# Unread products and a four-bank score rotation in the last head group of a macaron transformer layer

## The reference

```
x = x + 0.5 * ffn(ln(x))
x = x + attn(ln(x))          # 16 heads of 16, rotary embedding, causal softmax, output projection
x = x + 0.5 * ffn(ln(x))     # the same weights as the first

ffn(u):  prev = u shifted by one row, zeros first
         xk = mu_k*u + (1-mu_k)*prev ;  xr = mu_r*u + (1-mu_r)*prev
         k = xk @ W_k.T ; r = sigmoid(xr @ W_r.T)
         return r * (square(relu(k)) @ W_v.T)
```

## Time and profile before

| | |
|---|---|
| median of 3 runs | 3127.63 us (3127.12 to 3133.78) |
| profiled execution, its own time | 3128.23 us |
| its span, first to last instruction | 3126.5 us |
| mean granted TensorE clock | 0.986 |
| PE busy over the span | 2973.8 us, 95% |
| DVE, ACT, POOL busy over the span | 80%, 69%, 50% |

### The profile page before, as it was taken

The page is one execution under the profiler, slowest core; times in us unless marked ns, Lnnn a source line. Parts: engine busy times, 40 slices in busy tenths (PEclk is TensorE's granted clock), DMA queues, the critical chain, the costliest instruction groups (busy, mean ns, idle before and its releaser), DMA issues.

```text
span 3126.5 us, 57247 instructions
## 1 busy us (share of the span) xinstructions
PE 2973.8 (95%) x18245; PEld 1667.7 (53%) x18245; DVE 2511.6 (80%) x8326; ACT 2159.5 (69%) x4802; POOL 1566.1 (50%) x2190
## 2 busy tenths in 40 slices
PE   6899999999999999999999999999999999999987
PEld 5444555555555555555555555555555555555434
DVE  3888888888888888888888888888888888888862
ACT  4476677776777777777776777777777676777664
POOL 5455455555454455555555455455555555454322
PEclk8899999999999999999999999999999999999998
DMA  3443243443334253343343334243343433343411
GB/s 99 78 86 65 63 98 68 85 88 75 83 76 91 64 100 73 69 97 68 85 88 74 83 77 92 64 100 74 69 96 69 83 88 75 83 76 79 78 45 38
DMA packets 202593, 245.56 MB, mean 79 GB/s; under 512 B 68405, under 2 KB 104245, under 8 KB 202293
## 3 DMA queue, kind: packets, MB, share of 16 engines
q1 hardware_dynamic: 202293, 241.90, 37.3%
HBM read 53.48 MB, written 51.38 MB: 34 GB/s over the span
## 4 chain that ended last, share of the span: by engine, by line
PE 69%; DVE 15%; ACT 7%; issue 4%; POOL 3%; DMA 1%; SPq 1%; POOLq 0%; DVEq 0%; ACTq 0%
PE ps_y L720 15%; PE ps_s L689 13%; PE ps_m L699 11%; DVE ps_m L926 7%; PE ps_d L779 7%; PE ps_d L773 6%; PE ps_d L785 5%; PE ps_d L776 5%; ACT pt_sb L815 4%; PE ps_d L766 3%; PE ps_d L727 2%; PE ps_d L789 2%; DVE dif_sb L956 1%; DVE ka_sb L950 1%; DVE sw_sb L979 1%
## 5 line engine op out<-in xcount | busy, mean ns | idle before, releaser
L815 ACT ACTIVATE pt_sb<-ps_s 128x512 f32<-128x512 f32 (+3 forms) x3072 | 1464.8, 494 | 839.8 <-PE ps_s L689 829.7
L926 DVE CUSTOM_DVE_ANT_0 ps_m<-ps_m,mask_sb 128x512 f32<-128x512 f32 (+3 forms) x3072 | 1676.1, 570 | 446.9 <-PE ps_m L699 429.7
L689 PE MATMUL ps_s<-qr_sb,kr_sb 99*128 99x512 bf16 (+3 forms) x3072 | 1008.2, 331 | 55.1 <-ACT pt_sb L815 42.7
L699 PE MATMUL ps_m<-kr_sb,qr_sb 96*128 96x512 bf16 (+3 forms) x3072 | 1000.5, 329 | 42.6 <-DVE mx_sb L926 38.0
L1057 POOL TENSOR_SCALAR_AFFINE_SELECT pt_sb<-pt_sb 128x512 f32<-128x512 f32 x512 | 330.7, 646 | 845.1 <-ACT pt_sb L815 844.1
L720 PE MATMUL ps_y<-pt_sb,v_sb 128*32 128x512 f32 (+3 forms) x6144 | 593.4, 496 | 1.2 <-POOL pt_sb L1057 1.2
L689 PEld LDWEIGHTS ps_s<-qr_sb,kr_sb 99*128 99x128 bf16 x3072 | 294.8, 96 | 527.2 <-issue 233.8
L699 PEld LDWEIGHTS ps_m<-kr_sb,qr_sb 96*128 96x128 bf16 x3072 | 302.0, 98 | 325.9 <-DVE mx_sb L926 96.9
L926 DVE DVE_READ_ACCUMULATOR2_ANT mx_sb<- 128x1 f32 x3072 | 431.6, 140 | 0.0
L785 PE MATMUL ps_d<-axn_sb,wqk_sb 128*128 128x256 f32 x1024 | 306.1, 397 | 4.0 <-ACT axn_sb L857 3.9
L773 PE MATMUL ps_d<-ka_sb,wk_sb 128*128 128x256 f32 x1024 | 305.6, 395 | 1.0 <-DVE ka_sb L950 0.9
(11 more groups left out here) (92 smaller groups left out, 3273.7 us busy)
## 6 DMA issues: line engine op xcount, KB each, us to landing
kr_sb<-part_sb SPq DMA_DIRECT2D x378, 128.0 KB, 4.4
qr_sb<-part_sb SPq DMA_DIRECT2D x378, 128.0 KB, 4.7
y_way<-yt_sb SPq DMA_DIRECT2D x128, 256.0 KB, 2.7
sw_sb<-qb_sb SPq DMA_DIRECT2D x496, 64.0 KB, 2.0
x_sb<-x SPq DMA_DIRECT2D x64, 256.0 KB, 2.8
yn_sb<-y_way SPq DMA_DIRECT2D x64, 256.0 KB
den_sb<-r_way SPq DMA_DIRECT2D x64, 256.0 KB
out<-x_sb SPq DMA_DIRECT2D x64, 256.0 KB, 2.2
```

Of the source, the lines that this page charges most:

```text
L689: eng.matmul(ps_s[:, slot % NS, 0:width], kr_sb[0:KR + NP, n % RS, j, kb * P:(kb + 1) * P], qr_sb[0:KR + NP, n % RS, j, q0:q0 + width], st ...
L699: eng.matmul(ps_m[:, u % NM, 0:width], qr_sb[0:KR, n % RS, j, i * P:(i + 1) * P], kr_sb[0:KR, n % RS, j, piece * QC:piece * QC + width], s ...
L815: eng.activation(pt_sb[:, buffer, j, column:column + width], ps_s[:, slot % NS, 0:width], ACT.Exp, scale=SCALE).then_inc(exped, 1)
L926: eng.tensor_tensor_reduce(ps_m[:, u % NM, 0:width], ps_m[:, u % NM, 0:width], mask_sb[:, m0:m0 + width], 1.0, -3e38, ALU.add, ALU.max, mx ...
```

## The change

In the last group and the eight slots ahead of it (from slot 3016, `LONE`), the scores go round four banks, the two of `ps_s` and the first two of `ps_m`, so that a score waits for the exponential of four slots before. The third bank of `ps_m` takes products that nobody reads: `keep_going(n)` issues n matmuls of the form of `f_K` (128 x 128 by 128 x 256, fp32). There is one ahead of each score from slot 3016 on (56), four behind T124 and T126, two behind T125 and T127, and six behind the last matmul of p_P 63. In the planner, the lags of the last batch element's chunks 124 and 125 are halved, `xp` counts as one slot's lag for all four chunks, and p_P 62 and 63 are due at slots 3036 and 3038 with a lag of 1 behind `y_mul`, which ranks them ahead of the feed-forward steps. The outputs are computed as before.

```diff
-            came = ("xp", i, 2) if second else ("load", i, 8 if b else 0)
+            came = ("xp", i, 1 if b == nb - 1 else 2) if second else ("load", i, 8 if b else 0)
+            near = (lambda lag: math.ceil(lag * 0.5)) if second and b == nb - 1 and c < NCH // 2 else (lambda lag: lag)
...
-            s("POOL", "f_rstd", p, 1.3, t, ("f_st1", p, 3), ("f_x1", p - 2, 1))
-            s("ACT", "f_x0", p, 0.36, t, ("f_rstd", p, 4))
+            s("POOL", "f_rstd", p, 1.3, t, ("f_st1", p, near(3)), ("f_x1", p - 2, 1))
+            s("ACT", "f_x0", p, 0.36, t, ("f_rstd", p, near(4)))
...
-            s("PE", "f_T", p, 0.5, t, ("f_x1", p, 2))
+            s("PE", "f_T", p, 0.5, t, ("f_x1", p, near(2)))
...
-                t = (b + 1) * BSLOTS - 16 + 8 * c + 12 * (c // 2)
-                s("PE", "p_P", i, 4, t, ("y_mul", NQC * (b * NP2 + NP2 - 1) + c // 2, 3))
+                last = b == nb - 1 and c >= NCH // 2
+                t = nb * BSLOTS - 40 + 2 * c if last else (b + 1) * BSLOTS - 16 + 8 * c + 12 * (c // 2)
+                s("PE", "p_P", i, 4, t, ("y_mul", NQC * (b * NP2 + NP2 - 1) + c // 2, 1 if last else 3))
...
+        LONE = n_ticks * G - GSLOTS - 8
+        N_LONE = NS + NM - 1
+
+        def score_bank(slot):
+
+            if slot < LONE:
+                return ps_s[:, slot % NS, :]
+            at = (slot - LONE) % N_LONE
+            return ps_s[:, at, :] if at < NS else ps_m[:, at - NS, :]
...
-                pe.wait_ge(exped, slot - NS + 1)
-                eng.matmul(ps_s[:, slot % NS, 0:width], kr_sb[0:KR + NP, n % RS, j, kb * P:(kb + 1) * P],
+                if slot < LONE + NS:
+                    pe.wait_ge(exped, slot - NS + 1)
+                elif slot < LONE + N_LONE:
+                    pe.wait_ge(max_taken, n_groups * NU)
+                else:
+                    pe.wait_ge(exped, slot - N_LONE + 1)
+                eng.matmul(score_bank(slot)[:, 0:width], kr_sb[0:KR + NP, n % RS, j, kb * P:(kb + 1) * P],
...
+            def keep_going(times):
+
+                pe.wait_ge(max_taken, n_groups * NU)
+                for _ in range(times):
+                    eng.matmul(ps_m[:, NM - 1, 0:C], wk_sb[:, 0, 0:P], wk_sb[:, 1, :], start=True, stop=True)
...
                 if name == "f_T":
                     pe.wait_ge(f_xt, CT * (i + 1))
                     transposes(ps, xt_sb).then_inc(made[d], 1)
+                    b, c, second = plan.ffn[i]
+                    if second and b == nb - 1:
+                        keep_going(2 if c % 2 else 4)
                     return
...
                     if u == CT * NP2 - 1:
                         mm.then_inc(made[d], 1)
+                        if i == nb * NCH - 1:
+                            keep_going(6)
...
                 if slot in SCORE_AT:
+                    if slot >= n_ticks * G - GSLOTS - 8:
+                        keep_going(1)
                     score(SCORE_AT[slot])
```

More of the change, by code:

```diff
@@ L129, in describe @@
             i = b * NCH + c
-            came = ("xp", i, 2) if second else ("load", i, 8 if b else 0)
+            came = ("xp", i, 1 if b == nb - 1 else 2) if second else ("load", i, 8 if b else 0)
+            near = (lambda lag: math.ceil(lag * 0.5)) if second and b == nb - 1 and c < NCH // 2 else (lambda lag: lag)
             s("DVE", "f_st0", p, 0.33, t, came, ("f_st1", p - 1, 0))
             s("DVE", "f_st1", p, 0.51, t, ("f_st0", p, 0), ("f_x1", p - 2, 1))
-            s("POOL", "f_rstd", p, 1.3, t, ("f_st1", p, 3), ("f_x1", p - 2, 1))
-            s("ACT", "f_x0", p, 0.36, t, ("f_rstd", p, 4))
+            s("POOL", "f_rstd", p, 1.3, t, ("f_st1", p, near(3)), ("f_x1", p - 2, 1))
+            s("ACT", "f_x0", p, 0.36, t, ("f_rstd", p, near(4)))
             s("ACT", "f_x1", p, 0.36, t, ("f_x0", p, 0))
-            s("PE", "f_T", p, 0.5, t, ("f_x1", p, 2))
+            s("PE", "f_T", p, 0.5, t, ("f_x1", p, near(2)))
             s("ACT", "f_xn", p, 0.48, t, ("f_T", p, 1), ("f_r1", p - 2, 1), ("f_dif", p - 1, 1))
-            s("POOL", "f_dif", p, 1.2, t, ("f_xn", p, 2), ("f_R", p - 2, 1), ("f_xadd", p - 2, 1))
-            s("DVE", "f_k0", p, 0.62, t, ("f_dif", p, 2), ("f_V", p - 2, 1))
+            s("POOL", "f_dif", p, 1.2, t, ("f_xn", p, near(2)), ("f_R", p - 2, 1), ("f_xadd", p - 2, 1))
+            s("DVE", "f_k0", p, 0.62, t, ("f_dif", p, near(2)), ("f_V", p - 2, 1))
             s("DVE", "f_k1", p, 0.62, t, ("f_k0", p, 0))
@@ L142, in describe @@
             s("DVE", "f_r1", p, 0.46, t, ("f_r0", p, 0))
-            s("PE", "f_K", p, 4, t, ("f_k1", p, 3))
+            s("PE", "f_K", p, 4, t, ("f_k1", p, near(3)))
             s("ACT", "f_relu", p, 0.5, t, ("f_K", p, 1))
             s("ACT", "f_sq", p, 0.55, t, ("f_relu", p, 0))
-            s("PE", "f_R", p, 4, t, ("f_K", p, 0), ("f_r1", p, 3))
+            s("PE", "f_R", p, 4, t, ("f_K", p, 0), ("f_r1", p, near(3)))
             s("ACT", "f_tanh", p, 0.47, t, ("f_R", p, 1))
-            s("PE", "f_V", p, 4, t, ("f_R", p, 0), ("f_sq", p, 2))
-            s("DVE", "f_u", p, 0.61, t, ("f_V", p, 1), ("f_tanh", p, 2))
-            s("POOL", "f_xadd", p, 1.2, t, ("f_u", p, 2))
+            s("PE", "f_V", p, 4, t, ("f_R", p, 0), ("f_sq", p, near(2)))
+            s("DVE", "f_u", p, 0.61, t, ("f_V", p, 1), ("f_tanh", p, near(2)))
+            s("POOL", "f_xadd", p, 1.2, t, ("f_u", p, near(2)))
             if second:
@@ L814, in exponential @@
                 act.wait_ge(pved, done)
-                eng.activation(pt_sb[:, buffer, j, column:column + width], ps_s[:, slot % NS, 0:width], ACT.Exp, scale=SCALE).then_inc(exped, 1)
+                eng.activation(pt_sb[:, buffer, j, column:column + width], score_bank(slot)[:, 0:width], ACT.Exp, scale=SCALE).then_inc(exped, 1)
             def dense(name, i):
```

## The result

The changed kernel takes 3133.61 us (median of 13 runs, 3129.55 to 3137.81) against 3126.93 us for the kernel before in the same sessions (13 runs, 3122.89 to 3133.78). The ratio is 1.0024 with a 95% interval of 1.0017 to 1.0032: slower by 0.24%, some 7 us. That is just beyond the 0.2% that the prediction called the limit, and the interval still holds that limit: slower than before is clear of the noise, beyond 0.2% is not. The profiled execution took 3137.81 us, its span is 3136.1 us, the mean granted clock 0.992 (0.986 before).

A forecast was written before the change was run, and what follows sets the result against it. Slow clock and bursts starving ACT bound the last group, then the tail. The last burst moving +6.9 us, less 5.0 from reordering and other tail terms, gave span +2.5, time 3130.1 us; 8-in-10 range 3123.5 to 3137.5.

The forecast's parts named there:

- The likeliest case: Whole kernel: no change within 0.2% (6.3 us), leaning slow, own range 3126 to 3133 us; chance 0.76.
- P: Start of the last burst of `pv`: forecast at 3088.5 us, 6.9 later than in the kernel before.
- Part 1: Scores from slot 3016: with an unread product ahead of each, PE becomes the bound, 46.7 us of work against 43.1.
- Part 2: Scores of the last group: four banks give 0, as ACT is no longer the bound; bounds 0 to 0.5 us.
- Part 3: End of the last group: T124 and its four unread products stand ahead of the last burst, delaying it 3.3 us.
- Part 4: Tail: p_P 62 comes directly behind K125, worth 5.0 us of the last burst's delay; K126 at 3113.6, span 3129.0.
- A: Last group: filling costs nothing, the last burst stays at 3081.6, time 3120.1; chance 0.07 with all other big gains.
- B: Last group: clock still falls, 18 us at 0.50 move the last burst by another 9 us, time 3139; chance 0.12.
- C: Tail: p_P 62 lands ahead of K125 (+1.8 us, time 3131.9) or stays behind V125 (as forecast); chance 0.15.

The follow-up runs named there:

- half_group_fill: Changed kernel with 128 columns in place of 256 in each of the 56 unread products ahead of the scores: 3122.7 us, ratio 0.9986 to the kernel before.
- two_banks_fill: Changed kernel with its scores back in two banks, all unread products and the new order kept: 3136.4 us, ratio 1.0025 to the kernel before.
- no_p63_fill: Changed kernel without the six unread products behind p_P 63: 3132.3 us, ratio 1.0017 to the kernel before.
- old_order: Changed kernel with the planner of before, all unread products and four banks kept: 3130.8 us, ratio 1.0008 to the kernel before.
- no_group_fill: Changed kernel without the 56 unread products ahead of the scores: 3116.0 us, ratio 0.9965 to the kernel before.
- banks_order: Kernel before plus four banks, unread products only behind the four transposes, p_P 62 and 63 between K125 and R125: 3111.7 us, ratio 0.9950.
- banks_tail_fill: Kernel before plus four banks and unread products only behind the four transposes, old order: 3114.5 us, ratio 0.9953.
- banks_only: Kernel before plus the four-bank rotation alone, no unread products, old planner: 3117.8 us, ratio 0.9969.
- lean: Changed kernel without unread products ahead of scores, behind T124 or behind p_P 63: 3115.8 us, ratio 0.9955 to the kernel before.

## Why the prediction held, and where it was short

The range held (3123.5 to 3137.5, measured 3133.61) and the direction it leaned to was right. The likeliest case was missed narrowly: its own range ended at 3133, and the ratio lies on the slow side of the 0.2% limit, which had 0.17, though the interval does not exclude the limit. The mechanism was the forecast one; the terms were too small by 3.8 us together, from the first unread product (3041.75) to the end 94.35 us where I had 90.5. P came at 3094.03, where 3088.5 was forecast and 3086 to 3090 was its range. 3.3 us of the difference is the body, which ended later in this execution, and 2.3 us are the terms: counted from the first unread product, P lies at 52.3 us, also past the upper bound of 51.0.

**Part 1, the unread products as PE time: right, mis-sized by 2.2.** The forecast was 46.7 us of PE work up to slot 3071 (46.6 when summed anew, since 56 x 0.43 is 24.1), measured 48.9 (3041.75 to 3090.69). The unread product costs 0.435 and the scores are as priced. What was missing stands between products of different kinds. Around a burst: 0.20 from the last score to it (3043.93 to 3044.13) where the score costs 0.12, and 0.54 for the unread product behind it (3045.77 to 3046.31) in place of 0.43. With eight bursts that is 1.5 of the 2.2. Behind a score of 128 columns: 0.49 for the unread product (3046.37 to 3046.85), so that a narrow slot costs 0.54 and not 0.49; with eleven such places that is 0.6. I had given each kind one price. Two of the three dearer distances could be read in the trace of the kernel before: a product of this form in front of a burst took 0.52 there, and one behind a score of 128 columns 0.49.

```profile
3009.52 0.65 PE L776 MATMUL ps_d<-wr_sb,dif_sb 128*128 128x256 f32 x2
3010.01 0.22 PE L689 MATMUL ps_s<-qr_sb,kr_sb 99*128 99x128 bf16 x1
...
3013.66 0.60 PE L779 MATMUL ps_d<-wv_sb,ka_sb 128*128 128x256 f32 x2
3014.18 0.86 PE L720 MATMUL ps_y<-pt_sb,v_sb 128*32 128x256 f32 x16
```

That PE and not ACT is the bound, and that the clock holds, came out (half_group_fill, 0.20 us for each half).

**Part 2, four banks are worth 0 here: right** (two_banks_fill, 0.1 us). The prediction stopped there. It didn't say what they are worth without part 1, though its rows gave ACT 0.54 a slot and PE less than that; it is the most valuable part of the change.

**Part 3, T124 ahead of the last burst: right.** T124 came 1.1 us behind the last score (1.2 forecast) and P 2.3 behind T124's start (2.2).

**Part 4: the order right, three terms short.** `y_mul` 63 ended at P+12.3, not P+11.7. What it waited for last was the DMA to `den_sb`, and in the second profile of the same kernel it ended at P+11.6: these 0.6 us are a chance of one execution. (The P+16.8 from which I counted the gain of the new order is the chain's start of p_P 62; PE's timeline of the kernel before has it at 3098.25, P+16.6.) T126 came 9.8 us behind p_P 62 (9.6 forecast). From T126 to K126 it took 4.45 us, not 3.69: a wait that I had not listed. `f_xadd` 125 stands ahead of `f_dif` 126 in POOL's list, as before, but with V125 moved behind p_P 63, right in front of T126, it is ready only then. The six unread products are not the reason, since no_p63_fill has the same 4.44 us; with the old planner the distance is 3.7 again (old_order). POOL's timeline of the changed kernel:

```profile
3117.11 1.28 POOL L1115 TENSOR_TENSOR x_sb<-x_sb,dif_sb 128x512 f32<-128x512 f32 x1 [3.46 <-DVE dif_sb L992]
3118.32 0.20 POOL L1107 COPY fxn_sb<-fxn_sb 128x2 f32<-128x2 f32 x1
3118.60 1.04 POOL L1110 TENSOR_TENSOR dif_sb<-fxn_sb 128x512 f32<-128x512 f32 x1
```

K126 to the end took 15.4 us, as forecast.

**The rivals.** A (the filling costs nothing) fell: P moved by 9.1 us against M. B (the clock still falls) fell: in all six kernels with an unread product ahead of each score that clock never left 1.00 between M and P. Without the filling, all of the profiles with four banks have less of the fall than both with two (0.76 and 0.88 between M and P): 1.00 in no_group_fill, banks_order and banks_tail_fill, 0.95 in banks_only and lean. The Trainium skill (TensorE: Matmul & The Clock Gate, "A second HAM failure mode: psum-queue depth-cycling") tells of a kernel whose products cycle through PSUM banks and whose clock swings, and the prediction took from it that four banks would keep the fall. The trace agrees in part: two of the five profiles with four banks have one fall of some 3 us, three have none. C (p_P lands elsewhere in the list) didn't occur: the list was the one worked out.

## What to carry to other kernels

An instruction that is there to keep a clock up is work like any other: price it against the slack of its own slot, and put it only where the engine would idle anyway (here behind the transposes of the tail, some 4 us won), never ahead of each step of a loop that another engine paces (17 us lost). When a change bundles a part that frees an engine with one that loads it, cost each alone as well; here the bundle was 7 us slower, and one of its parts alone 10 us faster. When work is moved in a list executed in order, look on every engine for what is queued in front of the next critical step, such as a tanh or an add of the chunk before.

## What the runs showed of the hardware that was not expected

- The distance that a matmul costs depends on its neighbours. Around a burst of four 128 x 32 products side by side it is 0.08 to 0.09 us more in front and 0.11 more behind, and an fp32 product behind a bf16 one of 128 columns costs 0.49 us in place of 0.43. Prices taken from one pair of kinds are too low by that for another. Why is not shown.
- The kernel before had its granted clock at 0.50 for 20 us of the last group in one profile and for 10 us, in other places, in the next, with stretches of 42.6 and 41.7 us (a mean of 0.76 and 0.88 between the levels 0.50 and 1.00). Here, how long the clock was low is a poor measure of what it cost; the estimate above puts that down to ACT waiting or not in those moments.
- The clock fell in some profiles and held in others over the same instructions. Up to the last burst banks_only and banks_tail_fill are one program, and in the 6 us around M PE was busy 5.00 us in both. Then the clock fell for some 3 us in banks_only and held 1.00 in banks_tail_fill. What decides it is not shown.

```profile
3033.00:3039.00 6.00, 5.00 (x34) 1.48 (x36) 3.17 (x11) 4.43 (x12) 1.27 (x2) 1.00 0.01 1
3033.40:3039.40 6.00, 5.00 (x33) 1.50 (x36) 3.15 (x11) 4.43 (x12) 1.27 (x2) 1.00 0.00 1
```

The first of these windows is of banks_only, the second of banks_tail_fill.
